# Moving z1's norm, the context scores and their exponent to other places of a software-pipelined slot

## The reference

```python
x = x + xattn(layernorm(x), ctx)
    # sa = attention(y, y, y, causal); y = layernorm(y + sa, g1, beta1)          -> z1, y1
    # ca = attention(y, Z, Z);         y = layernorm(y + ca, g2, beta2)          -> z2, y2
    # ff = relu(y @ w1 + b1) @ w2 + b2; y = layernorm(y + ff, g3, beta3)          -> z3
x = x + ffn(layernorm(x))
    # q(v): per block of 16, scale = max|v| / 6; v / scale to the nearest of
    #       0, .5, 1, 1.5, 2, 3, 4, 6 (with sign); times scale
    # h = silu(q(x) @ q(w_gate).T) * (q(x) @ q(w_up).T);  out = q(h) @ q(w_down).T
```

## Time and profile before

| what | value |
|---|---|
| median of 3 runs | 600.66 us (599.99 to 603.07) |
| the profiled execution | 600.61 us |
| its span, first to last instruction | 598.5 us |
| TensorE busy | 563.8 us, 94% |
| VectorE, GpSimd, ScalarE busy | 495.5, 385.8, 374.6 us |
| mean granted TensorE clock | 0.989 |

### The profile page before, as it was taken

One profiled execution on the slowest core, in us unless ns is written; L12 is line 12 of the kernel. 1 busy time (PEld: TensorE's weight loads), 2 busy tenths in 40 slices (PEclk: granted clock), 3 DMA queues, 4 the chain that ended last, 5 costly groups with the idle time before them and its releaser, 6 DMA issues.

```text
span 598.5 us, 12474 instructions
## 1 busy us (share of the span) xinstructions
PE 563.8 (94%) x4054; PEld 535.5 (89%) x4054; DVE 495.5 (83%) x1220; ACT 374.6 (63%) x779; POOL 385.8 (64%) x466
## 2 busy tenths in 40 slices
PE   4798879999999999999999999999999999999886
PEld 2677779999999999999999999999999999999785
DVE  4889898887988888887988888887988878877775
ACT  3666575766667575766667674866667674757231
POOL 3657667676767667675767666666767666675543
PEclk9797999999999999999999999999999999999999
DMA  7701010010201010010101010010201010000000
GB/s 228 241 2 37 0 28 19 1 55 1 62 1 55 2 34 30 0 53 0 61 0 53 0 42 19 0 53 0 61 2 35 3 36 1 19 2 19 0 10 27
DMA packets 18743, 19.31 MB, mean 32 GB/s; under 512 B 1536, under 2 KB 18192, under 8 KB 18704
## 3 DMA queue, kind: packets, MB, share of 16 engines
q1 hardware_dynamic: 18704, 18.82, 10.4%
HBM read 14.62 MB, written 4.19 MB: 31 GB/s over the span
## 4 chain that ended last, share of the span: by engine, by line
PE 73%; DVE 6%; POOL 5%; issue 5%; ACT 2%; POOLq 0%; DVEq 0%; ACTq 0%
PE R L1124 6%; PE R L1126 6%; PE R L1125 6%; PE O L1176 5%; PE TR L1029 5%; PE O L1239 4%; PE R L1194 4%; PE R L1196 4%; PE R L1195 4%; PE O L1241 4%; PE O L1240 4%; PE O L1218 3%; PE O L1220 3%; PE O L1219 3%; PE R L1029 3%
## 5 line engine op out<-in xcount | busy, mean ns | idle before, releaser
L461 POOL TENSOR_TENSOR rs<-mv,neg_half 128x1 f32<-128x1 f32 (+1 forms) x112 | 68.2, 619 | 32.1 <-DVE mv L1589 30.9
L1124 PE MATMUL R<-gu_hi,xqT_hi 128*128 128x352 f32 x240 | 80.2, 334 | 2.9 <-ACT hT L743 2.0
L1194 PE MATMUL R<-y2T_hi,w_hi 128*128 128x256 f32 x256 | 77.5, 303 | 4.6 <-ACT e_diag L777 1.7
L754 ACT ACTIVATE hqT_hi<-R 128x768 fp32r<-128x768 f32 x29 | 23.6, 812 | 86.8 <-PE R L1029 86.8
L1126 PE MATMUL R<-gu_hi,xqT_lo 128*128 128x352 f32 x240 | 77.3, 322 | 0.0
L1125 PE MATMUL R<-gu_lo,xqT_hi 128*128 128x352 f32 x240 | 77.2, 322 | 0.0
L1239 PE MATMUL O<-w_hi,hT_hi 128*128 128x256 f32 x256 | 74.5, 291 | 0.9 <-POOL hT_lo L496 0.9
L1196 PE MATMUL R<-y2T_hi,w_lo 128*128 128x256 f32 x256 | 73.2, 286 | 0.0
L1195 PE MATMUL R<-y2T_lo,w_hi 128*128 128x256 f32 x256 | 73.1, 285 | 0.0
L1241 PE MATMUL O<-w_hi,hT_lo 128*128 128x256 f32 x256 | 71.9, 281 | 0.0
L1240 PE MATMUL O<-w_lo,hT_hi 128*128 128x256 f32 x256 | 71.7, 280 | 0.0
(11 more groups left out here) (197 smaller groups left out, 1830.7 us busy)
## 6 DMA issues: line engine op xcount, KB each, us to landing
x_in<-in_x SPq DMA_DIRECT2D x16, 256.0 KB, 2.9
x_res<-in_x SPq DMA_DIRECT2D x16, 256.0 KB, 2.8
out<-x SPq DMA_DIRECT2D x32, 128.0 KB, 1.9
ctx_rows<-in_ctx SPq DMA_DIRECT2D x16, 64.0 KB, 2.5
hT<-in_L_xattn_w SPq DMA_DIRECT2D x1, 1024.0 KB, 7.3
hh<-in_L_xattn_w SPq DMA_DIRECT2D x1, 768.0 KB, 8.7
wd_raw<-in_L_ffn_w_down SPq DMA_DIRECT2D x1, 704.0 KB, 9.4
w_raw<-in_L_ffn_w_gate SPq DMA_DIRECT2D x1, 640.0 KB, 4.4
```

Source lines behind the costliest of these rows:

```text
L1124: mm(o, xh, gu_hi[:, c, m, cols], start=(c == 0), stop=False)
L1194: mm(o, w1_hi[:, c, cols], y2T_hi[:, c, :], start=(c == 0), stop=False)
```

## The change

On TensorE y0's transposes stand one ff1 block earlier, z1's transposes right behind the scores of the self-attention instead of ahead of the last gate_up group, the context scores ahead of the last gate_up group instead of behind it, and the second ff2's turn of h comes after four column blocks instead of two. On ScalarE z1's norm and the copies of its transposes move forward to the scores; the exponent of the context scores stands behind the last Silu and ahead of |h|, no longer behind |h|; z2's norm stands ahead of h's high part. On VectorE z1's statistics and shift move forward, `ff_sum(b, h, 0)` stands behind `h_scale` and `h_reciprocal`, and z2's shift directly behind its statistics. On GpSimd the powers and the rows of y1 move forward accordingly. No operation is added or removed. The diff, cut to its core:

```diff
-        FF2_TURN = FC // 4
+        FF2_TURN = FC // 2
...
 (GpSimd slot)
                 if f1:
                     gamma3(b, g, 0)
                     x1_sum(b, g, 0)
+                    power(3, b, g, F, (1,))
                 if q1:
                     unscale_h(b, g, 1)
...
+                if a:
+                    power(1, b, h, A, (0, 1))
+                if f1:
+                    scale_x(b, g, 0)
+                    power(4, b, g, F, (1,))
                     unscale_x(b, g, 0)
-                    power(4, b, g, F, (1,))
+                    scale_x(b, g, 1)
...
+                if a:
+                    y_rows(b, h, True, 0)
+                    y_rows(b, h, True, 1)
                 if f:
                     y_rows(b, h, False, 0)
                     y_rows(b, h, False, 1)
...
 (ScalarE slot)
                 if front:
                     copy_y0T(b, h)
+                if a:
+                    norm(1, b, h, A, 0, 1, z1[:, 0, :], z1[:, 0, :])
+                    norm(1, b, h, A, 1, 1, z1[:, 1, :], z1[:, 1, :])
...
                     exp_scores(b, h)
                     exp_rest(b, h)
+                if a:
+                    affine_turned(b, h, A, n1_turned, y1T, g1_col, beta1_col, y1T_set)
...
                 if q:
-                    silu(b, h, 1, (0,))
+                    silu(b, h, 1, (0, 1))
                 if a:
-                    affine_turned(b, h, A, n1_turned, y1T, g1_col, beta1_col, y1T_set)
+                    if q:
+                        warm(b, h, ACT.Exp, 1)
+                    exp_cross(b, h)
                 if q:
-                    silu(b, h, 1, (1,))
                     abs_h(b, h, 0)
                 if f and not a:
                     return
-                if q:
-                    warm(b, h, ACT.Exp, 1)
                 if a:
-                    exp_cross(b, h)
                     cp_upper(b, h)
+                    norm(2, b, h, A, 0, 1, z2[:, 0, :], z2[:, 0, :])
+                    norm(2, b, h, A, 1, 1, z2[:, 1, :], z2[:, 1, :])
                 if q:
                     hT_upper(b, h, 0)
...
                     abs_h(b, h, 1)
-                if a:
-                    norm(2, b, h, A, 0, 1, z2[:, 0, :], z2[:, 0, :])
-                    norm(2, b, h, A, 1, 1, z2[:, 1, :], z2[:, 1, :])
...
 (TensorE slot)
-                if f:
-                    ff1(b, h, (1,))
                 if front:
                     turn_y0(b, h)
                 if f:
-                    ff1(b, h, (2, 3))
+                    ff1(b, h, (1, 2, 3))
                 if front:
                     ready_for_scores(b, h)
                     scores(b, h)
                     scores_rest(b, h, range(T))
+                if a:
+                    turn_z1(b, h)
...
                     gate_up(b, h, 1, 0)
                 if a:
-                    turn_z1(b, h)
+                    cross(b, h)
                 if q:
                     gate_up(b, h, 1, 1)
-                if a:
-                    cross(b, h)
...
 (VectorE slot)
-                    self_reciprocal(b, h, 1)
-                    self_sum(b, h, 1)
+                    self_part(b, h, 1)
+                    self_stats(b, h)
...
+                if a:
+                    shift(1, b, h, A, (0, 1))
...
-                if q:
-                    h_product(b, h, 1, 1)
                 if a:
                     cross_max(b, h)
                 if q:
+                    h_product(b, h, 1, 1)
                     h_lift(b, h, 0)
                     h_drop(b, h, 0)
                     h_max(b, h, 1)
...
                     cp_lower(b, h)
                     cross_reciprocal(b, h)
-                if f:
-                    ff_sum(b, h, 0)
                 if q:
                     h_scale(b, h, 1)
                     h_reciprocal(b, h, 1)
+                if f:
+                    ff_sum(b, h, 0)
                 if a:
                     cross_sum(b, h)
-                if a:
-                    wait(dve, z2_set, b, h, A, T, T)
-                    stats(2, b, h, A, 0, z2)
-                    stats(2, b, h, A, 1, z2)
-                    aggregate(2, b, h, A, 0)
-                    aggregate(2, b, h, A, 1)
+                    cross_stats(b, h)
+                    shift(2, b, h, A, (0, 1))
                 if f:
                     z3_stats(b, h, 0)
                     aggregate(3, b, h, F, 0)
-                if a:
-                    shift(2, b, h, A, (0, 1))
...
```

## The result

| kernel | median us | ratio to before, 95% interval |
|---|---|---|
| before | 601.35 | |
| after | 687.49 (684.78 to 689.64) | 1.142 (1.139 to 1.145) |

What follows compares the result with a forecast made beforehand. The prediction took TensorE's own work to bound each slot, so only its waits count. It summed 600.6 + 38.9 (first stall) + 14 (second values) + 18 (rest of the margins) = 671.5 us, range 634 to 694.

Steps and rivals of the forecast that it cites:

- the pause: Sign of being right: TensorE idle for about 2.4 us ahead of the context values, at each of 14 slots.
- VectorE's idle time: Sign of being right: VectorE idle for nearly 2 us ahead of its rounding step, ended by ScalarE's |h|.
- The waits of 0.7 and 1.6 us ahead of the second values: Sign of being right: TensorE waits 0.7 and 1.6 us in turn there.
- a clock below 1 in the middle: Sign of being wrong: TensorE's granted clock below 1 in the middle of the span.
- The bound: A slot of about 33.5 us is as long as TensorE's own work; whatever makes TensorE wait lengthens it.
- The first stall: Late |h| delays VectorE's context-weight low part and freeing sum; TensorE 2.78 us later in 14 slots, 38.9 us.
- The second values: TensorE waits there for a late accumulator-freeing sum, 0.74 or 1.6 us by kind of slot; taken as 14 us.
- The rest of the margins: y2's low part, z1's forward chain and work behind it run late: 1.3 us in 14 slots, 18 us.
- h's transposes behind four instead of two ff2 columns: TensorE's later place for these transposes costs nothing, as the unscaling they wait for also comes later.
- The clock: Rival, chance 0.20: TensorE's granted clock also falls behind the new pauses, +14 us, so 685 us (675 to 710).
- first stall alone: Rival, chance 0.17: the chain through |h| holds but its followers are hidden; 639.5 us (632 to 655).
- faster: Rival, chance 0.03: the |h| chain misses the context weights' low part and old waits go; 595 us.

Runs made afterwards that it cites:

- e1: The changed kernel with one step undone: on ScalarE |h| stands ahead of the table load and context exponents again; 661.64 us, ratio 1.098.
- e7: e1 with the context scores on TensorE behind the last gate_up group again and their maximum on VectorE behind the last product; 657.45 us.
- e8: e1 with the sum that frees the accumulator for ff2's second half ahead of h's scale and reciprocal again on VectorE; 660.73 us.
- e2: The kernel before with one step of the change alone: on ScalarE |h| stands behind the context exponents; 634.82 us, ratio 1.056.
- e10: e9 with |h| behind the context exponents again, as in the changed kernel; 662.77 us, ratio 1.101.
- e12: e2 with seven extra 512-column matmuls, results not used, in the pause ahead of the context values; 623.54 us, ratio 1.037.
- e4: The changed kernel with nine extra 512-column matmuls, results not used, ahead of the context values; 686.68 us, ratio 1.140.
- e6: e1 with h's second low part on VectorE moved ahead of x's norm and block maximum; 656.24 us, ratio 1.093.
- e11: e9 with z1's statistics, power, norms, affine and transposes also back where they stood before; 622.02 us, ratio 1.035.
- e5: e1 with z2's two norms on ScalarE behind h's high part and the second |h| again; 643.58 us, ratio 1.072.
- e9: The changed kernel with five steps undone: |h| early, z2's norms late, h's second low part early, context scores late, freeing sum early; 631.70 us.

## Why the prediction was right, and where not

The time lies in the range, and just inside the forecast's own (655 to 688), 16 us above the sum. Of the signs named for it, the pause, VectorE's idle time (1.81 us), the end of |h|, the share of TensorE (86%) and, nearly, the slot (39.5 us, half of the 79.1 below) came. The waits of 0.7 and 1.6 us ahead of the second values did not come (2.7 us in four places), and a clock below 1 in the middle, which it had named as a sign of being wrong, did.

**The bound** held. Every new wait of TensorE came on top. Two slots take 79.1 us, from the context values at 294.42 to those at 373.51, where the earlier trace rows had 67.

**The first stall** was right in its parts. Silu to the end of |h| took 2.86 us (2.96 foreseen), the low part started 2.64 behind the first rounding step (2.63), the pause was 2.29 (2.4), and the second ff2 waited 5.9 / 13 = 0.45 (0.55). But 14 x 2.78 = 38.9 us is not what it costs. The term is made of three steps of the change: |h| behind the exponents, the earlier context scores (0.81) and the late sum (0.55). Undone, they gave 25.8 (e1) and, on top of it, 4.2 (e7) and 0.9 (e8), together 30.9, although e1 waits 7.4 us for that sum: where one of them does not delay TensorE, other waits do. |h| behind the exponents alone costs 33.5 (e2) and 31.1 (e10), each with the clock's share, and 22.7 with the pause filled (e12). The step that failed is the multiplication: it counted the delay as if no other wait gave any of it back.

**The second values.** The wait was foreseen at the right place and nearly in size: 14.8 us by the working, 10.6 in e1. But the working hung it on the late sum of the first stall, and e1, without that stall, has it all the same. Its cause is the other half of that paragraph, z2's norm ahead of h's high part on ScalarE. Undoing that gave 18.1 us against the 14 taken. In the changed kernel itself only 2.7 us show, and 10.5 in e4 with the clock back at 1.00: the slow matmuls use up the rest.

**The rest of the margins** was too small: 18 us, at most 35. e1 stands 60.3 above before; without the 18.1 of z2's norm and the 5.1 of the scores and the sum, 37.1 are left for it, more than its upper bound. The wait of the scores was not named at all. VectorE's rows of the changed kernel show it: z1's statistics and aggregate, and x's norm and maximum, stand ahead of h's second low part, which ends at 351.07, while TensorE comes to the scores 0.93 ahead of 351.22.

```profile
348.06 0.76 DVE L1588 BATCH_NORM_STATS2 st<-z 128x6 f32<-128x256 f32 x2
348.74 0.42 DVE L1592 BATCH_NORM_AGGREGATE mv<-st 128x2 f32<-128x9 f32 x2
349.08 0.67 DVE L1706 TENSOR_SCALAR w_raw<-w_raw,mv,rs 128x256 f32<-128x256 f32 x1
349.79 0.42 DVE L1609 TENSOR_REDUCE x_amax<-w_raw 128x16 f32<-128x256 f32 x1
350.12 0.95 DVE L1677 TENSOR_TENSOR hqT_lo<-R,hqT_hi 128x768 fp32r<-128x768 f32 x1
```

The place of h's low part is worth 5.4 (e6) and z1's place 9.7 (e11). The 21 us that stay in e11 are not divided by a run, and their cause stays open. One part of them can be read from rows, and it is a term that the prediction put at nothing: h's transposes behind four instead of two ff2 columns. In the kernel before they start 0.93 us behind the first matmul of the second ff2, and z2's transposes follow without a wait:

```profile
262.58 0.39 PE L1236 MATMUL O<-shift_parts,ones 128*128 128x256 f32 x1
263.51 0.82 PE L1029 MATMUL R<-ident,hq 128*128 128x128 f32 x6
267.36 0.66 PE L1029 MATMUL TR<-ident,w_raw 128*128 128x128 f32 x4
```

In e11 they start 1.66 us behind it, and h's high part, |h| and z2's norm follow them in ScalarE's queue. z2's transposes now wait for that norm, by about as much as h's transposes are later (0.73 us):

```profile
268.20 0.39 PE L1243 MATMUL O<-shift_parts,ones 128*128 128x256 f32 x1
269.86 0.82 PE L1036 MATMUL R<-ident,hq 128*128 128x128 f32 x6
273.71 0.66 PE L1036 MATMUL TR<-ident,w_raw 128*128 128x128 f32 x4 [0.72 <-ACT w_raw L713]
```

By these rows this is the wait in every second slot of e11 (5.5 us in 7 places), and e5 and e9 list the same one. No run undid the step by itself, so its price is not shown.

The three terms were 38.9, 14 and 18; by these runs they are 30.9, 18.1 and 37.1, together 86.1. The forecast was near because one was too large and two too small, which is luck in part.

**The clock** fell, behind 11 of 14 pauses, as the rival had it and the forecast not, and the rival's 685 us lies nearest to the time. But its price was wrong: 14 us net there, 0.8 in e4. Its own remark, that a slower TensorE uses up the followers' waits, held to almost the full amount. That 687 is near 685 is therefore no proof of the rival: the 16 us above the sum come from the rest of the margins, less what the first stall was too large.

**The other rivals** fell: first stall alone (632 to 655) with e1, where 60 us stay without that stall, and faster with the order of ScalarE's rows, where |h| ends 2.86 us behind the last Silu.

## What to carry to other kernels

When an instruction that waits is moved forward in a queue that runs in order, look at what stands behind it and is ready: here a norm that waited for its shift held back a copy, and through it the saturated engine, in every slot. Price each such place as a wait of its own, and test it by undoing it alone and together with the others, since a single undo shows only what the next wait does not take (e6 half, e8 nothing). A clock that fell cost 11.3 us where the engine had no other recurring wait (e2 against e12) and 0.8 where it had (e4); a filler in the pause tells the two cases apart.

## What the runs showed of the hardware

I had not expected pauses this short to bring the clock down in a kernel whose TensorE is busy for most of every slot. In e2, with pauses of at most 1.8 us, the stretch behind 7 of 14 has a clock below 1. Two neighbouring pauses (the 4 us from the start of the context values):

```profile
239.70:243.70 4.00, 3.63 (x19) 3.56 (x20) 3.61 (x13) 0.01 (x1) 2.49 (x3) 0.65 0.02 4
276.10:280.10 4.00, 3.67 (x28) 3.36 (x29) 3.58 (x13) 1.26 (x4) 2.49 (x3) 1.00 0.00 0
```

The one has 19 matmuls of TensorE and the other 28; the first had 1.2 GHz, the lower level, for a part of the time. The length of the pause does not decide by itself: the 14 pauses of the changed kernel are alike (32.0 us in all, 2.3 at most), and behind three of them the clock stayed at 1.00. What decides is not shown here. In e1, whose longest recurring wait is 1.0 us, the clock stayed at 1.00 from 100 to 560 us.
